# One GNN, attention and expert block: keys of the linear attention multiplied once, with features on partitions

## The reference, cut to what matters

```python
xn = _layernorm(x, axis=-1)
# graph part: segment_sum over edges of (xn @ W)[src] * norm, then a norm over all values, PReLU
out = segment_sum(h[src_f] * norm[:, None], dst_f, num_segments=n) + conv_bias
...
# attention part, 4 heads of 32, 4 memory keys and values
xn = rmsnorm(x, g_pre)
q, k, v = split(xn @ w_qkv, 3)
k = concatenate([mk, k], axis=-1); v = concatenate([mv, v], axis=-1)
q = softmax(q, axis=-2) * SCALE        # over the 32 features of a head
k = softmax(k, axis=-1)                # over all nodes
context = einsum('bhdn,bhen->bhde', k, v)
out = einsum('bhde,bhdn->bhen', context, q)
out = rmsnorm(out @ w_out + b_out, g_out) + x
...
# then x = x + experts(layernorm(x))
```

## Time and profile before

| what | value |
|---|---|
| median of 3 runs | 1326.18 us (1324.99 to 1328.23) |
| the profiled execution's own time | 1320.53 us |
| its span, first to last instruction | 1318.8 us |
| TensorE busy | 1206.9 us (92%) |
| VectorE busy | 911.9 us (69%) |
| GpSimd busy | 789.1 us (60%) |
| ScalarE busy | 543.8 us (41%) |
| mean granted TensorE clock | 0.965 of full speed |

### The profile page before, as it was taken

How to read it: one execution, slowest core, us unless ns; L and a number is a source line. 1 busy time by engine, 2 the same in 40 slices (tenths; PEclk the granted TensorE clock), 3 DMA queues, 4 the chain that set the end, 5 groups by cost and what they waited for, 6 DMA issues and landing times.

```text
span 1318.8 us, 29769 instructions
## 1 busy us (share of the span) xinstructions
PE 1206.9 (92%) x8357; PEld 1076.2 (82%) x8358; DVE 911.9 (69%) x2764; ACT 543.8 (41%) x1403; POOL 789.1 (60%) x757
## 2 busy tenths in 40 slices
PE   6974989998999999998998798958999999999998
PEld 6964978887889888887786646945999999999997
DVE  8997987887888778778784268888444444444444
ACT  8837102222333333333321102645555555555553
POOL 7105777777777777777777300003577666667665
PEclk9997999999999999999999899965999999999999
DMA  8026333336666667779998701578354444444443
GB/s 256 0 78 199 100 104 105 103 104 198 193 194 205 195 197 210 207 239 276 281 295 271 259 0 33 176 238 249 57 77 65 70 71 71 70 69 70 69 68 43
DMA packets 138889, 190.10 MB, mean 144 GB/s; under 512 B 22262, under 2 KB 116957, under 8 KB 138533
## 3 DMA queue, kind: packets, MB, share of 16 engines
q0 software_dynamic: 43440, 90.29, 29.6%
q1 hardware_dynamic: 95348, 98.64, 23.6%
HBM read 156.37 MB, written 33.44 MB: 144 GB/s over the span
## 4 chain that ended last, share of the span: by engine, by line
PE 54%; POOL 14%; DVE 9%; issue 7%; DMA 4%; DVEq 2%; ACT 1%; SPq 0%; POOLq 0%
PE ps L1991 14%; PE ps L2001 14%; POOL RG L811 14%; PE ps L828 7%; PE ps L851 4%; PE ps L1534 3%; DMA zrow<-table 2%; PE ps L1571 2%; PE ps L1981 2%; DVE R L1088 2%; PE ps L874 1%; PE ps L1589 1%; DMA RG<-table,srci 1%; PE ps L839 1%; DVEq L1080 1%
## 5 line engine op out<-in xcount | busy, mean ns | idle before, releaser
L811 POOL DMA_INDIRECT RG<-table,srci x476 | 468.4, 984 | 146.8 <-issue 142.9
L828 PEld LDWEIGHTS ps<-S_t,RG 128*128 128x128 f32 x1936 | 255.7, 196 | 21.5 <-DMA RG<-table,srci 11.4
L828 PE MATMUL ps<-S_t,RG 128*128 128x96 f32 x1936 | 258.9, 277 | 8.7 <-DMA RG<-table,srci 8.3
L851 PE MATMUL ps<-zrow,R 128*128 128x256 f32 (+1 forms) x784 | 220.8, 387 | 19.3 <-DMA zrow<-table 12.9
L2116 POOL DMA_INDIRECT out<-R,S_t x105 | 166.1, 1582 | 96.9 <-DVE R L2086 50.3
L1991 PE MATMUL ps<-R,RG 128*128 128x128 f32 x1680 | 204.9, 275 | 0.0
L2001 PE MATMUL ps<-R 128*128 x840 | 198.6, 380 | 0.0
L1991 PEld LDWEIGHTS ps<-R,RG 128*128 128x128 f32 x1680 | 195.9, 192 | 0.2 <-issue 0.2
L2028 ACT ACTIVATE R<-ps,RG 128x128 f32<-128x128 f32 x420 | 119.7, 368 | 177.1 <-PE ps L1991 177.1
L1088 DVE TENSOR_TENSOR R<-R,ps 128x245 f32 (+4 forms) x300 | 141.8, 473 | 69.4 <-PE ps L839 42.6
L2082 DVE TENSOR_TENSOR R<-ps,R 128x256 f32<-128x256 f32 x105 | 44.6, 425 | 202.0 <-PE ps L2001 202.0
(11 more groups left out here) (374 smaller groups left out, 1822.7 us busy)
## 6 DMA issues: line engine op xcount, KB each, us to landing
zrow<-table SPq DMA_DIRECT2D x384, 128.0 KB
RG<-table,srci POOLq DMA_INDIRECT x484, 3.3
ntable<-R SPq DMA_DIRECT2D x12, 516.0 KB, 6.6
out<-R SPq DMA_DIRECT2D x12, 512.0 KB, 3.2
table<-R SPq DMA_DIRECT2D x9, 640.0 KB
R<-in_x SPq DMA_DIRECT2D x6, 896.0 KB, 10.0
R<-in_w SPq DMA_DIRECT2D x8, 514.0 KB, 5.7
slot<-in_x SPq DMA_DIRECT2D x32, 128.0 KB
```

What stands on the lines that cost most here:

```text
L811: nc.gpsimd.indirect_dma_start(out=grows[:, s, :], out_offset=None, in_=table, in_offset=bass.IndirectOffsetOnAxis(ap=srci[:, ND + q, c:c ...
L828: last = nc.tensor.matmul(window(q % 2)[:, h, :], grows[:, s, h * P:(h + 1) * P], S_t[:, q % 2, c, :], start=c == 0, stop=c == GC - 1)
L851: nc.tensor.matmul(psD[:, 0:D], adj[b % 2][0:n, j, :], zrow[0:n, i % ZR, :], start=j == 0, stop=j == T - 1).then_inc(z_used, 1)
```

## The change

The keys are multiplied once. Four tiles (`KS = 4`, 13 rounds, `NKS`) go through one round of nine quarters (`KD = 9`, starting at quarter `K0 = 8`, which is turn 2; the last ends in turn 31): `keys(k)` makes keys with features on partitions for 512 nodes, VectorE scales them by a row of norms, reduces them to a maximum per feature and lowers the running `negM`; ScalarE exponentiates with that as bias, and makes `fade`, by which the context so far is to be scaled; TensorE turns the four tiles back (`turn_exp`), ScalarE copies them and the values out of PSUM, TensorE multiplies (`context`), VectorE adds to `ctx_s` in SBUF. The row of norms is got by a turn of `cq` at the start of the stage, a store to HBM and a spread load of it for each round into `zrow`. So SyncE's loads of table rows start after the last round. The clears of `adj` on ScalarE now stand behind the first exponent and the copy of that turn.

The queries start at turn 35, not 37. `EARLY` is 1: four gathers of the eight are now issued behind the barrier. The last block is turned behind the last aggregate, and added last.

```diff
+KS = 4
+NKS = -(-T // KS)
...
-        EARLY = 2
+        EARLY = 1
...
-        A0, A1 = 0, 12
-        C0, C1 = 14, 34
-        B0, B1 = 37, 88
+        K0, KD = 8, 9
+        C1 = 32
+        B0, B1 = 35, 88
...
+        def key_turn(q, r):
+
+            at = 4 * q + r - K0
+            return [(k, at - KD * k) for k in range(NKS) if 0 <= at - KD * k <= KD]
...
+                sp.wait_ge(cr_ok, 1)
+                sp.dma_start(cflat.rearrange("(t p) -> t p", p=P), ks4[0:T, 0:P]).then_inc(cr_out, 16)
+                sp.wait_ge(cr_out, 16)
+                for k in range(NKS):
+                    if k >= 2:
+                        sp.wait_ge(k_ok, k - 1)
+                    lo, n = KS * k * P, key_nodes(k)
+                    sp.dma_start(cq_row[k % 2][:, 0:n],
+                                 cflat[lo:lo + n].unsqueeze(0).to_broadcast([P, n])).then_inc(cr_in[k % 2], 16)
+                sp.wait_ge(cx_ok, NKS + 1)
                 for q in range(-2, GQ - 2):
...
+                def turn_exp(k):
+                    pe.wait_ge(ex_ok, k + 1)
+                    pe.wait_ge(k_top, k + 1)
...
+                def context(k):
+                    pe.wait_ge(et_ok, k + 1)
+                    pe.wait_ge(v_ok, key_tiles(k)[-1] + 1)
+                    pe.wait_ge(cx_ok, k + 1)
...
+                    if q == 0 and r == 0:
+                        nc.tensor.transpose(psT[0:T, :], cq[:, :], ident[:, :])
+                        pe.wait_ge(mem_ok, 1)
+                        nc.tensor.transpose(psKT[0:MEM, 0:P], emk, ident[:, :])
+                        nc.tensor.transpose(psKT[0:MEM, P:2 * P], mvv[:, :], ident[:, :]).then_inc(pre_pe, 1)
...
+                    for k, at in key_turn(q, r):
+                        if at == 0:
+                            if k == 0:
+                                pe.wait_ge(cr_ok, 1)
+                            keys(k)
+                        if 1 <= at <= len(key_tiles(k)):
+                            values(KS * k + at - 1)
+                        if at == 4:
+                            turn_exp(k)
+                        if at == 7:
+                            context(k)
...
+                turn_block(NDB - 1)
...
+                act.wait_ge(m_ok, 1)
+                act.activation(emk, mk[:, :], ACT.Exp, bias=negM[0]).then_inc(mem_ok, 1)
+                act.wait_ge(pre_pe, 1)
+                act.activation(ks4[0:T, 0:P], psT[0:T, :], ACT.Copy).then_inc(cr_ok, 1)
                 for b in range(2):
                     wipe(b, 0, T).then_inc(clear, 1)
...
+                def keys_scaled(k):
+                    n = key_nodes(k)
+                    v.wait_ge(k_ps, k + 1)
+                    v.wait_ge(cr_in[k % 2], k // 2 * 16 + 16)
+                    if k >= 1:
+                        v.wait_ge(et_ps, k)
+                    nc.vector.tensor_tensor(ks4[:, 0:n], psKT[:, 0:n], cq_row[k % 2][:, 0:n], ALU.mult).then_inc(k_ok, 1)
+                    v.wait_ge(k_ok, k + 1)
+                    nc.vector.tensor_reduce(ktop, ks4[:, 0:n], AX.X, ALU.max).then_inc(k_top, 1)
+                    v.wait_ge(k_top, k + 1)
+                    nc.vector.scalar_tensor_tensor(negM[(k + 1) % 2], ktop, -1.0, negM[k % 2], ALU.mult,
+                                                   ALU.min).then_inc(m_ok, 1)
...
                 for q in range(GQ):
-                    if q in USED[1:]:
+                    if q in USED[1:-1]:
                         add_block(blocks, q - 1)
                         blocks += 1
...
                 add(GQ - 1, blocks)
+                add_block(NDB - 1, GQ)
```

229 lines of the change are left out of this document (114 added, 115 removed).

## The result

The changed kernel takes 1338.0 us (median of five runs, 1331.8 to 1338.7) where the kernel before takes 1325.97 us (five runs, 1323.96 to 1328.23). The ratio is 1.0079 (95% interval 1.0053 to 1.0105): slower, by 7 to 14 us, best 10.5. The profiled execution took 1338.0 us at a span of 1336.0. My forecast of 1325.6 us (1320.5 to 1332.0), most likely no change, was wrong.

The account below looks back on a forecast made before the run. GpSimd's gathers were taken to set the middle stage's pace, with TensorE fitting within it. All terms were 0 except -0.6 us at the last block's turn, giving a median of 1325.6 us, range 1320.5 to 1332.

Parts of the forecast that it names:

- What bounds the kernel now: Middle stage: GpSimd's gathers set the pace; TensorE catches up, 8.3 us of waits for rows, so its earlier lateness is forgotten.
- The keys: Key rounds: TensorE needs 9.8 us plus 1.0 of waits, within 11.6 us of nine quarters; effect 0.
- TensorE's rounds overflow the turns: Slower rival, chance 0.12: key rounds above 12.2 us use up 7.3 us of room and hold GpSimd; 1334 or 1358 us.
- The start of the stage: Stage start: first `chunk_add` 1.7 us later, GpSimd loses 0 to 1.2 us at group 4, 0.6 as before; effect 0.
- A later start: Slower rival, chance 0.04: the clear comes 5 us later than forecast and GpSimd loses that; 1330.5 us.
- Four early gathers instead of eight: Barrier before the middle stage: other engines start 5.0 us earlier, GpSimd gains nothing; effect 0.
- The table rows: SyncE's loads held back until turn 31, first needed in turn 33, 10 us later; in time, effect 0.
- The queries: Queries in the middle stage start two turns earlier and are a little thinner; effect 0.
- The turn of the last block: Stage end: sum complete about 1.0 us sooner, at most 0.6 shows before the small weight loads land; effect -0.6 us.
- Shorter gathers: Faster rival, chance 0.14: a lighter VectorE shortens GpSimd's gathers from 125 to 300 us by up to 5.2 us; 1320.4.

Follow-up runs that it names:

- e4: Changed kernel with the first clear of `adj` moved ahead of the exponent of the memory keys and the copy of the norms: 1331.78 us, 1.0024 of before.
- e9: e4 without VectorE's product of the keys with their norms, so it computes something else: 1325.21 us, 0.9982 of before.
- e16: Changed kernel, clear left late, without VectorE's product of the keys with their norms (computes something else): 1328.76 us, 1.0017 of before.
- e5: e4 with the turn of the exponents, their copies, the context and its addition each one quarter later in a round: 1335.01 us, 1.0075 of before.
- e10: e4 with the round spread further, from the reduction in quarter 3 to the context's addition in quarter 10: 1338.65 us, 1.0092 of before.
- e13: Kernel before with its two clears in the other order and the first `chunk_add` behind both: 1331.34 us, 1.0042 of before.
- e14: Kernel before with four early gathers, the same kernel as e2 in another sitting: 1325.13 us, 0.9994 of before.
- e15: e4 with eight early gathers instead of four: 1335.75 us, 1.0077 of before.
- e3: Kernel before with the last block's turn and addition moved behind the last aggregate: 1329.99 us, 1.0003 of before.
- e2: Kernel before with four early gathers, nothing else: 1322.86 us, 0.9969 of before.

## Why the prediction was wrong

*What bounds the kernel now* had the first fault. That GpSimd sets the pace was right: it waited 2.4 us in all. But I took TensorE's 8.3 us of waits for gathered rows for the whole stage and wrote that its lateness is forgotten there, without asking where they lay. The waits of TensorE in the kernel before, 400 to 600 us:

```profile
PE ps L828 <- DMA RG<-table,srci: 6.1, 10, 1.3
```

Another 2.1 us come after 600, and up to 400 there is none. In 155 to 275 us TensorE was busy for 113.4 of 120 us and never waited for gathers. From group 14 to group 40 it ran level with GpSimd, within the ring's room. Ahead of that it had gained on GpSimd in one place, the first pass over the keys, up to group 12 (3.0 to 8.9 us of room), and the change does away with that pass. So each new microsecond of it had to be weighed against the room, and a microsecond by which GpSimd is held isn't won back, as GpSimd is the pace afterwards.

*The keys* is the first of two steps that failed; the start, below, is the other. With the clear first the new keys still cost 3.2 us (e4), and the late clear adds 7. I had 9.8 us of work and 1.0 of waits in a round. Measured in 155 to 275 us: 103.33/120 of 11.9 = 10.2 us of work (0.4 more), and 16.7/120 of 11.9 = 1.7 of waits. The 1.0 us that I expected before the context wasn't there. Instead the chain of 2.6 us before the turn, "so it is covered" by 4.2 us of TensorE's work, showed 1.1 us in 11 of 13 rounds, and the counts' waits for `chunk_add`, for which the sum had no term, 6.9 us in these 120. It was counted as if VectorE stood ready when TensorE ends the keys. But VectorE takes up the product behind its own `chunk_add`s: the passes of `keys` start at 180.05 and end at 182.23, and the product starts at 184.95. And the cover itself, halves and counts, can't all run: counts wait for `chunk_add`, which stands behind the same 1.5 us of VectorE. e9 and e16 show the product to be worth 5.6 and 8 us; e5 and e10 show that the wait isn't moved away by a quarter, only renamed. That e5 is slower than e4 and not level I can only argue: more of the wait falls on counts, on which the aggregates' order hangs too.

*TensorE's rounds overflow the turns*, the rival with 0.12, is what happened. Its threshold of 12.2 us a round took a reserve of 7.3 us for given at the first round, and its margin took 10.8 us for the round. The reserve was read at group 18 of the kernel before, where the trace does have 7.4; but it is earned there by group 12, and at group 4 it is 3.0. In the changed kernel it was 1.7 at group 4 and 0.3 at group 18, and then a round of 11.9 us against the 11.3 of nine gathers was enough. The rival said 1334 us for waits of 3 us in a round; waits of 1.7 gave 1338.

*The start of the stage* was mis-sized. I priced only what GpSimd loses at the gather of group 4, 0 to 1.2 us, and took 0. The chain itself was right by its steps, and 3.1 us later by the long first gather. But its price is TensorE's lateness at the first round, which nothing gives back here: 7 us by e4, 5.6 in the kernel before by e13. Only a part of that stands before the first `keys` (GpSimd waits 1.8 us there). My third rival, *A later start*, had the mechanism with 0.04 and 1330.5 us. The two that I held apart happened together.

*Four early gathers instead of eight*: 0 was right alone (e14) and wrong in company (e15, 7 us). The step said that the others start 5.0 us earlier, which e4 and e15 show (the first `keys` at 139.66 and 144.66), and then gave that no value.

*The table rows* and *The queries*: as forecast. No wait of GpSimd or TensorE is put down to table rows near turn 33, and 13.0 us of such waits in all stand against 12.9.

*The turn of the last block*: the mechanism was right, the wait of 1.41 us is gone. Its size was off: I took 7.6 us for the landing of the last small load and had 0.6 us left; it took 8.83, and `features` started 10.7 us after group 118's last pass where it was 9.8 before. Nothing was won (e3, 1.0003).

*Shorter gathers*: there is a trace of it. The groups of GpSimd from 125 to 300 us, against 978 ns in the earlier trace rows:

```profile
L849 POOL DMA_INDIRECT RG<-table,srci x133 | 128.1, 963 | 49.6 <-issue 38.4 <-PE ps L866 9.7 <-POOLq L89 1.4
```

15 ns on 133 gathers is 2.0 us; the time shows nothing of it. Only a part of it can be VectorE's: with the old keys the mean was 971 in e2 and e14 and 966 in e13, with the new ones 961 in e4. By the rule of the Trainium skill that the prediction named, on the page "SBUF — State Buffer", section "Who interferes with whom", the gain would be small; the row agrees in size, and doesn't separate the kinds of instruction.

Of what I had named as proof, the gaps above 0.3 us before gathers between 145 and 300 us are there: from 155 to 310 us GpSimd waits five times, 8.0 us in all. The miss is thus no matter of scatter. The keys' round (11.9 us for 10.8), the reserve at its start (1.7 us at group 4 for 7.3) and the price of the late clear (7 us for 0) were wrong in the same direction.

## What to carry to other kernels

Before calling a saving or a delay "off the path", find the stretch in which the follower waits for the pace-setter: a total over the stage doesn't show that there is none where the change is. Where there is none, work out the follower's round with its waits in it; TensorE went from 94% to 86% busy there and its round came out longer than GpSimd's nine gathers, and a late start, a late barrier and a product then counted nearly in full. A reserve read at one place in a stage is not the reserve at another: ask where it was earned, and whether the change takes that place away. A chain's cover is to be counted from when the next engine is free to take the piece up, not from when the piece is ready, and work that waits for that same engine is no cover. The Trainium skill, page "Perfetto Trace Analysis", section "Identifying the Most-Contended Engine", says to find the engine of highest occupancy and optimise it first, and to judge TensorE not by its busy time but by, among others, the busy share of its weight loads. By that measure TensorE was just ahead in the 120 us shown (PEld 101.45, against VectorE's 100.19 and GpSimd's 91.68 us); its weight loads fell to 88.23, and the kernel became slower. The pace was GpSimd's: with 28.6 us of issue gaps its 91.68 fill the 120 us. So the measurement asks for the gaps on each engine and who ends them before the ranking by occupancy.

## What the runs showed of the hardware

The first early gather, whose start is released by the table's stores, took 1.26 to 1.32 us in three of the profiles (of before, e2 and e13) and 4.55 to 4.86 us in the other fifteen, kernels of both kinds among them. It moves the barrier by 3.5 us, and so in part how profiles of this kernel compare. Beside it VectorE makes 17 copies of 128x512 (L654, after the change L657), from 112.5 to 118.3 us. They took 5.87 to 5.91 us in the three profiles with the short gather and 5.79 in all fifteen others, where the long gather ends about a microsecond after them. So one seems to hold the other, and which one goes first to decide; no run tests it.

The three small loads at the end of the stage landed 5.8, 6.1 and 8.8 us after their issue, against 4.0, 4.3 and 7.6; moved out of the way, they left the large load in their place.

TensorE's granted clock falls for some us in the middle of the rounds too. Two aggregates of eight passes from the timeline of the changed kernel:

```profile
178.19 1.86 PE L866 MATMUL ps<-S_t,RG 128*128 128x96 f32 x8
...
182.06 1.03 PE L866 MATMUL ps<-S_t,RG 128*128 128x96 f32 x8
```

The first ran at the lower of the two clocks (1.2 GHz; the mean granted clock of 174 to 184 us is 0.83), after three waits of 0.98, 0.48 and 1.03 us between 172 and 177 us, and the round around it, 166.37 to 180.05, took 13.7 us at a mean granted clock of 0.90, where the same round of e4 took 12.3 at 1.00. The change has a second such round, 261.59 to 275.55 (14.0 us at 0.90), and so has e4 (13.9 at 0.88). The falls of the clock thus have a share in the long rounds that no run here separates from the waits before them. In e4 the last `keys` comes 6.6 us sooner than in the change, of which 4.5 are the start.

The same kernel against the same one before came out at 0.9969 and at 0.9994 in two sittings of five rounds (e2, e14). The intervals overlap, but the first alone excluded 1; at differences under 0.3% one sitting is not proof.
